# An adaLN transformer block on one core: the FFN's residual addition on GpSimd, and two VectorE steps behind their slots' maxima

## What is computed

```
h = layernorm(x) * (1 + ca) + sa
x = x + ga * attention(h)                     # softmax(q k / 4 + 8 bias) v, then Wo
h = layernorm(x) * (1 + cb) + sb
x = x + gb * fp4_linear(silu(fp4_linear(h, w_gate)) * fp4_linear(h, w_up), w_down)

fp4_quant_dequant(x): in blocks of 16: scale = max|x| / 6; round x / scale to
    {0, .5, 1, 1.5, 2, 3, 4, 6}; times scale
```

## Time and profile before

| | |
|---|---|
| time, median of 3 runs | 3245.57 us (3244.96 to 3246.62) |
| the profiled execution's own time | 3244.53 us |
| its span | 3242.7 us |
| PE busy | 3100.3 us, 96% |
| VectorE busy | 2737.1 us, 84% |
| ScalarE busy | 2139.4 us, 66% |
| GpSimd busy | 1816.5 us, 56% |
| L1226, the FFN's residual addition on VectorE | 128 instructions |
| L1161, low half of the hidden transposes | 256 instructions |

### The profile page before, as it was taken

The page is one execution under the profiler, slowest core; times in us unless marked ns, Lnnn a source line. Parts: engine busy times, 40 slices in busy tenths (PEclk is TensorE's granted clock), DMA queues, the critical chain, the costliest instruction groups (busy, mean ns, idle before and its releaser), DMA issues.

```text
span 3242.7 us, 67050 instructions
## 1 busy us (share of the span) xinstructions
PE 3100.3 (96%) x22916; PEld 1930.0 (60%) x22916; DVE 2737.1 (84%) x7909; ACT 2139.4 (66%) x3518; POOL 1816.5 (56%) x2169
## 2 busy tenths in 40 slices
PE   5899999999999999999999999999999999999985
PEld 2346666666666666666666666666666666666555
DVE  5778888888888888888888888888888888888865
ACT  3666666666666766666766666676666676676652
POOL 4535556565555555555655555556555565555455
PEclk7999999999999999999999999999999999999997
DMA  8443334233334324324423423433433433442200
GB/s 183 84 79 66 66 84 82 66 73 68 73 79 84 72 64 75 74 69 84 79 56 80 74 65 85 81 67 72 68 75 77 84 72 64 76 74 61 42 22 14
DMA packets 199937, 236.25 MB, mean 73 GB/s; under 512 B 25664, under 2 KB 178400, under 8 KB 199568
## 3 DMA queue, kind: packets, MB, share of 16 engines
q1 hardware_dynamic: 199600, 231.96, 35.7%
HBM read 162.74 MB, written 67.31 MB: 71 GB/s over the span
## 4 chain that ended last, share of the span: by engine, by line
PE 82%; ACT 6%; issue 5%; DVE 4%; POOL 2%; DMA 1%; SPq 0%; DVEq 0%; POOLq 0%; ACTq 0%
PE ps_x L703 33%; PE rings L674 14%; PE ps_o L692 13%; PE rings L657 13%; PE rings L660 5%; ACT probs L852 1%; DVE rings L1108 1%; PE ps_x L747 1%; ACT x_in L835 1%; DVE hq_l L1161 1%; ACT h_h L835 1%; ACT hq_h L967 1%; PE ps_x L768 1%; PE ps_x L753 1%; PE ps_x L760 1%
## 5 line engine op out<-in xcount | busy, mean ns | idle before, releaser
L1108 DVE CUSTOM_DVE_ANT_0 rings<-rings,band_z 128x512 f32<-128x512 f32 x2048 | 1404.0, 691 | 64.9 <-PE rings L674 58.2
L852 ACT ACTIVATE probs<-rings 128x1024 f32<-128x1024 f32 x1024 | 1050.1, 1025 | 532.7 <-PE rings L660 525.6
L674 PE MATMUL rings<-k_rows,q_half 120*128 120x512 bf16 x2048 | 792.5, 388 | 56.1 <-DVE row_max L1108 46.3
L657 PE MATMUL rings<-q_half,k_rows 121*128 121x512 bf16 x2048 | 701.8, 383 | 13.9 <-ACT probs L852 10.1
L660 PEld LDWEIGHTS rings<-rev,band_t 128*128 128x128 f16 x5632 | 409.2, 98 | 299.0
L692 PE MATMUL ps_o<-probs,values 128*32 128x512 f32 x4096 | 545.6, 605 | 0.0
L674 PEld LDWEIGHTS rings<-k_rows,q_half 120*128 120x128 bf16 x2048 | 196.8, 96 | 540.4 <-DVE row_max L1108 426.9
L660 PE MATMUL rings<-rev,band_t 128*128 128x64 f16 x5632 | 500.3, 192 | 0.0
L703 PE MATMUL ps_x<-w_gu_h,xq_h 128*128 128x512 f32 (+1 forms) x768 | 356.5, 464 | 1.4 <-DVE xq_l L1153 1.4
L1405 POOL TENSOR_TENSOR hidden<-hidden,inv 128x704 f32<-128x704 f32 x128 | 178.4, 1394 | 315.6 <-DVE inv L1147 315.6
L1207 DVE SCALAR_TENSOR_TENSOR tanh<-tanh,ps_x 128x256 f32<-128x256 f32 (+1 forms) x384 | 152.2, 396 | 171.8 <-ACT tanh L963 170.6
(11 more groups left out here) (187 smaller groups left out, 6714.0 us busy)
## 6 DMA issues: line engine op xcount, KB each, us to landing
parts_dram<-parts SPq DMA_DIRECT2D x128, 384.0 KB, 2.3
q_half<-parts_dram SPq DMA_DIRECT2D x384, 128.0 KB, 4.5
k_rows<-parts_dram SPq DMA_DIRECT2D x384, 128.0 KB, 7.0
mod_rows<-mod_rows_dram SPq DMA_DIRECT2D x32, 640.0 KB, 3.8
x_in<-in_x SPq DMA_DIRECT2D x32, 512.0 KB, 5.0
x_mid<-in_x SPq DMA_DIRECT2D x128, 128.0 KB, 2.0
out<-x_mid SPq DMA_DIRECT2D x128, 128.0 KB, 2.2
probs<-in_wmod SPq DMA_DIRECT2D x1, 1536.0 KB, 6.6
```

What stands on the lines that cost most here:

```text
L657: mm(ps_s[:, bank, :], kr[0:ROW_MAX + 1, h, k0:k0 + P], qr[0:ROW_MAX + 1, :], start=True, stop=False)
L674: mm(ps_m[:, bank, :], q_of(b, h)[0:ROW_MAX, j * P:(j + 1) * P], k_rows[par][0:ROW_MAX, h, :], start=True, stop=True).then_inc(mscores_rea ...
L852: A(prob_pair(s, j), ps_s, ACT.Exp).then_inc(exp_done, 1)
L1108: v.tensor_tensor_reduce(ps, ps, band_z[:, bias:bias + S], 1.0, LOWEST, ALU.add, ALU.max, row_max[:, par, 4 * h + j:4 * h + j + 1]).then_i ...
```

## The change

VectorE no longer adds the gated FFN product to the residual. At (0, 0) it still multiplies by the gate (`gate_ffn`), and GpSimd adds, in the first slot of each group, behind its addition of the bias row to another tile (L1371) and in front of the three FP4 steps of the hidden tile (L1376, L1378, L1380). GpSimd waits there for the gated product (`gb`), and those that waited for `out` (VectorE's `add_attention`, ScalarE's tanh of chunk 1, SyncE's store) now wait for GpSimd. Two VectorE steps move inside their position, from in front of `reduce_max` to behind it: `low_of_hidden` part 0 at (2, 3), and `silu_times_up` of chunk 1 at (2, 0). The other chunks and part 1 stay where they were.

```diff
-            def add_ffn(it, s, part):
-
-                u = it.tile(s, 3)
-                if part == 0:
-                    ps = read_job(it.earlier(s), (s - 1) % 16, "down")
-                    if it.has_tile(s, 1):
-                        after(dve, f1_dve, it.tile(s, 1), "res")
-                    v.tensor_tensor(gated, ps[:, 0:D], mod_rows[:, it.par, 4, :], ALU.mult).then_inc(f3_dve.sem, 1)
-                else:
-                    after(dve, f3_dve, u, "gb")
-                    v.tensor_tensor(x_mid[:, s // 4, :], gated, x_mid[:, s // 4, :], ALU.add).then_inc(f3_dve.sem, 1)
+            def gate_ffn(it, s):
+
+                ps = read_job(it.earlier(s), (s - 1) % 16, "down")
+                if it.has_tile(s, 1):
+                    after(dve, f1_dve, it.tile(s, 1), "res")
+                v.tensor_tensor(gated, ps[:, 0:D], mod_rows[:, it.par, 4, :], ALU.mult).then_inc(f3_dve.sem, 1)
...
-                        if at in CHUNK_AT and it.has_tile(s, 1):
-                            c = CHUNK_AT[at]
-                            silu_times_up(it, s - 1 if c == 1 else s, c)
-                        if at in ((2, 3), (3, 0)) and it.has_tile(s, 2):
-                            low_of_hidden(it, s, r - 2)
-                        if at in ((0, 0), (0, 3)) and it.has_tile(s, 3):
-                            add_ffn(it, s, j // 3)
+                        if at in CHUNK_AT and it.has_tile(s, 1) and CHUNK_AT[at] != 1:
+                            silu_times_up(it, s, CHUNK_AT[at])
+                        if at == (3, 0) and it.has_tile(s, 2):
+                            low_of_hidden(it, s, 1)
+                        if at == (0, 0) and it.has_tile(s, 3):
+                            gate_ffn(it, s)
...
                         if n == -1 and (s, j) == (12, 2):
                             split_output_weights()
+                        if at == (2, 3) and it.has_tile(s, 2):
+                            low_of_hidden(it, s, 0)
+                        if at == (2, 0) and it.has_tile(s, 1):
+                            silu_times_up(it, s - 1, 1)
                         if it.has(2):
                             layer_norm_1(it, s, j)
...
                             q.tensor_tensor(x_mid[:, t, :], x_mid[:, t, :], mod_rows[:, rp, 1, :],
                                             ALU.add).then_inc(f1_pool.sem, 1)
+                        if it.has_tile(s, 3):
+                            after(pool, f3_dve, it.tile(s, 3), "gb")
+                            q.tensor_tensor(x_mid[:, g, :], gated, x_mid[:, g, :], ALU.add).then_inc(f3_dve.sem, 1)
                         if it.has_tile(s, 2):
```

## The result

| | before | after |
|---|---|---|
| median of 5 runs each | 3246.03 us (3244.96 to 3247.26) | 3230.25 us (3227.86 to 3230.74) |
| ratio, 95% interval | | 0.9947 [0.9936, 0.9959] |
| span of the profiled execution | 3242.7 us | 3228.4 us |
| period of a steady iteration, from maxima to maxima | 96.22 us | 95.66 us |

A forecast was written before the change was run, and what follows sets the result against it. PE was taken as the bound, with stalls in slots 7, 11 and 12; 28 x 0.60 = 16.8 us gained, 2 lost at the end, 0.3 small change: -15, so 3230 us (ratio 0.995), range 3209 to 3241.

The forecast's parts named there:

- Slot 11, 0.35 gained: Low half behind its slot's maximum: PE's second maxima of slot 11 comes earlier, 0.35 us gained, half of its 0.70 stall.
- Slot 12, 0.25 gained: Product behind slot 12's third maxima: ctx_l ends about 0.58 earlier, so the rest of the stall, 0.25 us, goes.
- Slot 7, nothing: Slot 7: no gain, since VectorE's scale stays blocked until GpSimd's L1365 ends; the first half's gain is waited off.
- the 0.08 us of margin: Slot 7: VectorE's scale, moved 0.61 earlier, still comes 0.08 us behind the start of GpSimd's L1365.
- The silu, zero to 0.15: SiLU chunk 1 behind its slot's maximum: zero for PE, at most 0.15 us an iteration gained.
- The addition, zero for PE: Residual addition moved from VectorE (L1226) to GpSimd: PE waits for none of this, zero.
- VectorE's saving is mostly paid back: L1178 meets running GpSimd instructions, its median going from 0.484 to about 1.2; some 83 us come back.
- Slot 5: hidden: Addition of slot 4 ends about 1640.6, L1175 stands at 1640.7 anyway; chain to LN2 shift hidden with 0.2 left.
- The end, 2 us lost: Last eight or so tiles, without attention around them: GpSimd's addition costs between 0 and 6 us, taken as 2.
- (a): Rival: slot 7 gains too, about 0.55 an iteration, if VectorE's scale arrives before GpSimd's instruction; 3215, chance 0.20.
- (b): Rival: the gain is given back, ScalarE's order absorbing slot 12's 0.25 and the end costing 6 us; 3241, chance 0.12.
- (c): Rival: slower, L1178 of slot 5 loses the port twice (decides over 2.3 us), about 1.1 an iteration; 3261, chance 0.06.

The follow-up runs named there:

- The port's release: Changed kernel, GpSimd's second h_l (L1365) of slot 7 waits until VectorE's scale (L1145) is done: 3222.13 us, ratio 0.9923; same edit in the kernel before: 3244.93 us.
- the extra additions: Changed kernel with one or two more 128x256 additions ahead of the moved one in slot 4: 3232.70 us with one, 3243.64 with two.

## Why the prediction was right, point by point

**Slot 11, 0.35 gained: it was 0.31.** The steps came as told: the maxima 1.00 behind the weighing, the exponential still behind ScalarE's high halves, the scores 0.06 behind its end (1672.55 to 1672.61), the next maxima 0.56 behind that.

**Slot 12, 0.25 gained: it was 0.18.** The forecast that the product would not wait failed by a little. The maxima starts at 1679.06, `ctx_l` ends at 1679.15 and the product starts at 1679.21, 0.15 behind its maxima where it was 0.37. VectorE's `ctx_l`:

```profile
1678.73 0.42 DVE L1153 TENSOR_TENSOR ctx_l<-ps_x,ctx_h 128x256 fp32r<-128x256 f32 x1 [0.64 <-ACT ctx_h L945]
```

Together 0.49 where I had 0.60. The silu's move, which I had at zero, made up for part of it, with 0.03 each at (10, 3) and (14, 3). The rest is some hundredths of either sign, such as 0.03 lost at (11, 2). All slots together make 0.56, and 28 x 0.56 = 15.6. So the mechanism was right and the sum about right, but that the time came out within 1 us of the 3230 is in part luck: a term too large by 0.11 met one too small by 0.08, and the end cost 0.6 us less than I had taken.

**Slot 7, nothing: it was nothing**, 6.507 to 6.510, by the mechanism named, with the 0.08 us of margin as read. The port's release shows it as the cause. But I wrote that all of what the first half gains is waited off in front of the last maxima. That is true of 0.34 of the 0.74; the other 0.40 was waited off before, at the scores, behind the exponential, the limiter that I had named for slot 11 and not for slot 7.

The Trainium skill has a rule for this (SBUF — State Buffer, section "SBUF: two separate sides"): if VectorE's instruction runs in a two-port mode or has two SBUF inputs (this against a GpSimd instruction that reads SBUF), then whichever of it and GpSimd's starts first has the shared pair to its end. The trace agrees on who waits, down to 0.08 us: the scale, second by that much, took 1.26 for 0.18 of work. The scale has one SBUF input, so by that rule it must run in such a mode, which no run here shows.

**The silu, zero to 0.15: 0.08** in the company of the low half, 0.04 alone, but not in the place that I had named: the 0.15 in front of slot 7 was waited off, as told, and what stayed came at (10, 3) and (14, 3). **The addition, zero for PE: zero**, 0.02 of a period alone.

**VectorE's saving is mostly paid back.** By the durations of the instructions: L1226's 133.3 us are gone, L1178 went from 70.1 to 137.1 us (I had 83 more, it was 67; the median is 1.111, not 1.2), the blocked scale of slot 7 costs 17 more (by the low half's move, not by the addition) and the 2048 row maxima (L1108) 8. With small changes elsewhere that leaves 42 us less. The page's busy time fell by 12, since it counts the time in which two instructions overlap once.

**Slot 5: hidden, but by another way than I wrote.** I took L1175 to stand there "for its own reasons". It waits for GpSimd's addition, 28 times and 11.0 us. By these rows it costs nothing, since L1377 starts at 1633.30, and L1178 behind L1175 would still meet it, and be held to its end, 0.4 earlier; I did not run this. The room on the maxima's side is what the extra additions measured: 0.73 fits, 1.46 does not. The other chain, to the LN2 shift, had 0.39 left where I had 0.2.

**The end, 2 us lost: 1.3 to 1.4.**

**The rivals.** (a), that slot 7 gains too, had its condition right, since freeing the scale does make slot 7 gain, but I priced it at 0.55 an iteration and 3215; the runs say 0.33 and 3222. I took the scale to be all that holds the second half of slot 7, while the exponential takes 0.40 there too, and the down products' bank, freed by ScalarE's `h_h` at 1648.58, is next behind the scale. (b) fell: ScalarE kept half of slot 11, as in the forecast, and no more. (c), L1178 losing the port twice, did not come. Its longest is 1.789 in the whole run, under the 2.3 from which it would decide; two more additions bring a loss in that place, but with L1178 still at 1.11, through its later start.

## What to carry to other kernels

Before an instruction is moved earlier, look at what the shared port holds at its new time: the scale came 0.61 us earlier and was blocked 0.62 longer, and part of the gain (0.37 us) could then be fetched by letting the short instruction go first. A stall behind an in-order engine is often a step that waits, standing ahead of one that is ready; after the swap, the next limiter is found in the same slot (here ScalarE's list), and moving a step of it that could wait was worth another 0.39 us an iteration. Work taken off a busy engine is worth what its followers on PE's path gain, here nothing, and it costs in the stretch where single tiles run alone. To tell which of several moves gave a gain, compare the same distance in the kernels with each part alone: the 0.03 at (10, 3) looked like the low half's and was the silu's.

## What was new about the hardware

- VectorE's scale, one operand of 44 columns and 0.18 us long, is held by a running GpSimd instruction to its end: 1.26 us in slot 7, and 0.57 in slot 11 once GpSimd was put there. It then ends 0.04 behind it; VectorE's addition L1178, of 256 columns with two operands in SBUF, ends 0.28 to 0.29 behind it.
- VectorE's next maximum, with one operand in PSUM, is not held: in slot 5 it starts at 1635.05 and takes 0.69, while GpSimd's L1379 runs from 1634.92 to 1636.51.
